# Attention rounds reordered head by head, parts stored once, expert weights loaded after the rounds

## What is computed

```python
h = _layernorm(x) * (1 + ca) + sa
qkv = h @ w_qkv + b_qkv                       # 16 heads of depth 8
q, k = _rope(q), _rope(k)
scores = einsum('bhtd,bhsd->bhts', q, k) / sqrt(8)
out = einsum('bhts,bhsd->bhtd', softmax(scores), v)
x = x + ga * (out @ w_fc + b_fc)
```

## Time and profile before

| | us |
|---|---|
| median of three runs | 1827.18 |
| the profiled execution, its own time | 1828.58 |
| its span, first to last instruction | 1826.5 |
| set-up and first rounds, to the first pass 1 | 0 to 42 |
| rounds 0 to 17 | 42 to 385 |
| experts and layer 1 | 392 to 1826.5 |

### The profile page before, as it was taken

The page is one execution under the profiler, slowest core; times in us unless marked ns, Lnnn a source line. Parts: engine busy times, 40 slices in busy tenths (PEclk is TensorE's granted clock), DMA queues, the critical chain, the costliest instruction groups (busy, mean ns, idle before and its releaser), DMA issues.

```text
span 1826.5 us, 25499 instructions
## 1 busy us (share of the span) xinstructions
PE 1659.0 (91%) x7212; PEld 1027.0 (56%) x7212; DVE 1366.2 (75%) x2636; ACT 819.6 (45%) x1533; POOL 691.8 (38%) x628
## 2 busy tenths in 40 slices
PE   3888888869989999999999999999998899899999
PEld 2455555446655656556665565655655555555555
DVE  4777777656979988979969889799698587544444
ACT  1566767657644234243352342533525543433333
POOL 2011111100002945928739469187394475000000
PEclk9989989989999999999999999999999999999999
DMA  6554445246575877677767666666671111111110
GB/s 199 152 157 129 119 111 152 89 125 215 180 207 188 222 205 204 210 209 214 215 189 203 187 188 197 189 197 204 190 194 52 41 47 52 35 57 53 52 52 23
DMA packets 172698, 269.49 MB, mean 148 GB/s; under 512 B 23748, under 2 KB 61981, under 8 KB 170053
## 3 DMA queue, kind: packets, MB, share of 16 engines
q1 hardware_dynamic: 168691, 266.33, 49.9%
q10 hardware_dynamic: 1874, 1.36, 0.2%
q0 software_dynamic: 2048, 0.79, 0.2%
HBM read 233.78 MB, written 34.62 MB: 147 GB/s over the span
## 4 chain that ended last, share of the span: by engine, by line
PE 36%; DVE 16%; issue 10%; POOL 10%; ACT 3%; DMA 3%; SPq 1%; DVEq 0%; POOLq 0%; ACTq 0%
PE psum L1528 10%; PE psum L1368 6%; POOL e_prod L1986 6%; PE psum L1370 6%; PE psum L1369 6%; PE psum L1383 5%; DVE psum L1897 4%; POOL e_phi L1986 3%; DVE e_hm L1900 2%; DVE e_vbar L1755 2%; DVE e_y L1755 1%; DVE e_state L1850 1%; DMA e_ring<-w_split 1%; PE psum L1462 1%; DMA rw<-rw_fm 1%
## 5 line engine op out<-in xcount | busy, mean ns | idle before, releaser
L1694 ACT ACTIVATE e_gu<-psum 128x512 f32<-128x512 f32 (+1 forms) x368 | 219.3, 598 | 545.5 <-PE psum L1370 284.3
L1368 PE MATMUL psum<-e_hhi,e_ring 128*128 128x512 f32 x704 | 434.0, 616 | 19.7 <-DMA e_ring<-w_split 11.5
L1383 PE MATMUL psum<-e_hm,w_d 128*128 128x512 f32 (+1 forms) x736 | 382.6, 601 | 15.0 <-DVE e_hm L1903 7.2
L1986 POOL TENSOR_TENSOR e_prod<-e_state,e_phi 128x512 f32<-128x512 f32 x256 | 353.4, 1417 | 2.4 <-POOL e_phi L1986 1.7
L1897 DVE TENSOR_TENSOR psum<-psum,rw 128x512 f32<-128x512 f32 x352 | 243.4, 692 | 90.9 <-PE psum L1370 85.1
L1935 DVE TENSOR_TENSOR e_hm<-psum,rw 128x512 f32<-128x512 f32 x256 | 174.6, 688 | 178.0 <-ACT psum L1722 176.9
L1369 PE MATMUL psum<-e_hhi,e_ring 128*128 128x512 f32 x704 | 279.0, 396 | 0.0
L1370 PE MATMUL psum<-e_hlo,e_ring 128*128 128x512 f32 x704 | 278.8, 396 | 0.0
L1900 DVE TENSOR_TENSOR e_hm<-psum,e_gu 128x512 f32<-128x512 f32 x352 | 243.5, 692 | 39.4 <-ACT e_gu L1694 15.7
L1528 PE MATMUL psum<-e_hm,w_gu 128*128 128x512 f32 x512 | 262.9, 598 | 6.6 <-DVE w_d L1916 5.5
L1722 ACT ACTIVATE psum<-psum 128x512 f32<-128x512 f32 x256 | 148.8, 582 | 254.7 <-PE psum L1370 238.8
(11 more groups left out here) (304 smaller groups left out, 2181.0 us busy)
## 6 DMA issues: line engine op xcount, KB each, us to landing
e_ring<-w_split SPq DMA_DIRECT2D x308, 256.0 KB, 4.2
rw<-rw_fm SPq DMA_DIRECT2D x192, 176.0 KB
qk_parts<-at_part SPq DMA_DIRECT2D x96, 192.0 KB, 3.1
rw<-gates_fm SPq DMA_DIRECT2D x72, 256.0 KB, 3.2
w_split<-e_ring SPq DMA_DIRECT2D x44, 256.0 KB, 2.7
rw<-rw_fm SPq DMA_DIRECT2D x64, 160.0 KB
at_qs<-qk_parts SPq DMA_DIRECT2D x16, 576.0 KB
at_ks<-qk_parts SPq DMA_DIRECT2D x16, 576.0 KB
```

Source lines behind the costliest of these rows:

```text
L1368: pe.matmul(out, w_hi, x_hi, start=first, stop=False)
L1383: mm = pe.matmul(ps[:, ACC, :], weights_at(T, WD + P * j, P)[0:rows(j), :], hm[0:rows(j), slot(j), :], start=(j == 0), stop=(j == HT - 1))
L1694: a(act_g[0:r, j % 2, :], ps[0:r, GB[j % 2], :], ACT.Silu).then_inc(silu_done, 1)
L1986: ins = tt(out[:, at], x[:, at], y[:, at], op)
```

## The change

Four things. PE's order: the scores of one head at a time, with one short piece between heads, where `pv` is cut in halves of eight matmuls and the eight output transposes in two fours. DVE and ACT follow: the normalized output is made before the maximum of head 7 and the split, the second rest after head 8, the third cut after the copy of the first maxima; ACT copies the output after exponent 2. SP's stores: each part is written once (two stores a round), and each stack is loaded by three DMAs of 24 rows; for `ks` each of them reads one part three times over, as a broadcast. The weights: no pieces in the rounds; all 16 are issued after SP's last round, once the last maxima rows are in. The cut diff:

```diff
-STACK_DMAS = 2
-OUT_DMAS = 2 * PARTS
+STACK_DMAS = 2 * PARTS
+OUT_DMAS = 2
-PIECE_ROUNDS = (0, 1, 2, 3, 13, 14, 15, 16)
...
 
-            def pv(m, j, g):
-
-                pe.wait_ge(exp_done, HEADS * m + GROUP * (g + 1))
-                if g == 0:
+            def pv(m, j, g, st):
+
+                if st == 0:
+                    pe.wait_ge(exp_done, HEADS * m + GROUP * (g + 1))
+                if g == 0 and st == 0:
                     pe.wait_ge(v_ready, m + 1)
...
                         pe.wait_ge(o_ready, m)
-                for st in range(2):
-                    for c in range(GROUP):
-                        h = GROUP * g + c
-                        mm = pe.matmul(o_ps[VW * c:VW * (c + 1), g * SEQ:(g + 1) * SEQ],
-                                       v1[:, j % BUFS, st, h, :], pt[:, h % (2 * GROUP), st, :],
-                                       start=(st == 0), stop=(st == 1), tile_position=(0, VW * c))
-                mm.then_inc(pv_done, 1)
+                for c in range(GROUP):
+                    h = GROUP * g + c
+                    mm = pe.matmul(o_ps[VW * c:VW * (c + 1), g * SEQ:(g + 1) * SEQ],
+                                   v1[:, j % BUFS, st, h, :], pt[:, h % (2 * GROUP), st, :],
+                                   start=(st == 0), stop=(st == 1), tile_position=(0, VW * c))
+                if st == 1:
+                    mm.then_inc(pv_done, 1)
 
...
                     mm.then_inc(qk_proj, 1)
-                scores(n, k, 0, 0)
-                if k == BATCH:
-                    pe.wait_ge(r0_x, 1)
-                    pe.wait_ge(max_done, HEADS * BATCH)
-                    r0_ln.pe_x(pe)
+                scores(n, k, 0)
                 if f["p1"] or f["p2"]:
...
                     mm.then_inc(vn_done, 1)
+                scores(n, k, 1)
+                if k == BATCH:
+                    pe.wait_ge(r0_x, 1)
+                    pe.wait_ge(max_done, HEADS * BATCH)
+                    r0_ln.pe_x(pe)
                 if f["tail"]:
-                    pv(n - 2, k - 2, GROUPS - 1)
-                scores(n, k, 0, 1)
+                    pv(n - 2, k - 2, GROUPS - 1, 0)
+                scores(n, k, 2)
+                if f["tail"]:
+                    pv(n - 2, k - 2, GROUPS - 1, 1)
+                scores(n, k, 3, 4)
 
...
                     for tt in range(2):
+                        if tt == 1:
+                            scores(n, k, 5)
                         for g in range(GROUPS):
...
                     mm.then_inc(ot_done, 1)
-                scores(n, k, 1)
+                    scores(n, k, 6)
+                else:
+                    scores(n, k, 5, 6)
+                if f["p2"]:
+                    pv(n - 1, k - 1, 0, 0)
+                scores(n, k, 7)
                 if k == BATCH:
...
                 if f["p2"]:
-                    pv(n - 1, k - 1, 0)
-
-                scores(n, k, 2, 0)
+                    pv(n - 1, k - 1, 0, 1)
+                scores(n, k, 8, 9)
                 if f["p1"] or f["xn"]:
...
                     mm.then_inc(xt_done, 1)
-                scores(n, k, 2, 1)
+                scores(n, k, 10)
+                if f["p2"]:
+                    pv(n - 1, k - 1, 1, 0)
+                scores(n, k, 11)
                 if k == BATCH:
...
                 if f["p2"]:
-                    pv(n - 1, k - 1, 1)
+                    pv(n - 1, k - 1, 1, 1)
+                scores(n, k, 12)
 
...
                     mm.then_inc(at_done, 1)
-                scores(n, k, 3)
+                scores(n, k, 13)
                 if f["p2"]:
-                    pv(n - 1, k - 1, 2)
+                    pv(n - 1, k - 1, 2, 0)
+                scores(n, k, 14)
+                if f["p2"]:
+                    pv(n - 1, k - 1, 2, 1)
+                scores(n, k, 15)
                 if f["tail"]:
...
 
-            def maxima(n, k, g):
+            def maxima(n, k, first, end):
                 if not live(k)["p1"]:
                     return
-                for h in range(GROUP * g, GROUP * (g + 1)):
+                for h in range(first, end):
                     dve.wait_ge(p1_done, HEADS * n + h + 1)
...
                         .then_inc(qk_ready, 1)
-                maxima(n, k, 0)
+                maxima(n, k, 0, 4)
                 if f["proj"]:
...
                     nc.vector.tensor_tensor(rest[:], qk[:], part[:, 0, :], ALU.subtract).then_inc(rest_ready, 1)
-                maxima(n, k, 1)
-                split_maxima(n, k, 0)
-                if f["proj"]:
-                    dve.wait_ge(part_ready, PARTS * (n + 2) + 2)
-                    nc.vector.tensor_tensor(rest2[:], rest[:], part[:, 1, :], ALU.subtract).then_inc(rest_ready, 1)
+                maxima(n, k, 4, 7)
                 if k == BATCH:
...
                                             ALU.mult).then_inc(a_ready, 1)
+                maxima(n, k, 7, 8)
+                split_maxima(n, k, 0)
+                maxima(n, k, 8, 9)
+                if f["proj"]:
+                    dve.wait_ge(part_ready, PARTS * (n + 2) + 2)
+                    nc.vector.tensor_tensor(rest2[:], rest[:], part[:, 1, :], ALU.subtract).then_inc(rest_ready, 1)
                 if k == BATCH:
...
                         route_stage(nc.vector, r0_steps, r0_bufs, T["gate_b"], CT, stage, r0_weighted)
-                maxima(n, k, 2)
-                maxima(n, k, 3)
+                maxima(n, k, 9, HEADS)
                 split_maxima(n, k, 1)
...
         def _(act):
-            def exps(n, k, g, part=None):
-
-                for h in heads(g, part):
+            def exps(n, k, *run_of_heads):
+
+                for h in run_of_heads:
                     act.wait_ge(p2_done, HEADS * n + h + 1)
-                    if h % GROUP == 0 and (k > 0 or g >= 2):
-
-                        act.wait_ge(pv_done, GROUPS * n + g - 1)
+                    if h % GROUP == 0 and (k > 0 or h >= 2 * GROUP):
+
+                        act.wait_ge(pv_done, GROUPS * n + h // GROUP - 1)
                     nc.scalar.activation(pt[:, h % (2 * GROUP), :, :].rearrange("p s t -> p (s t)"), ps[:, P2[h % 2], :],
...
                 if f["p2"]:
-                    exps(n - 1, k - 1, 0, 0)
+                    exps(n - 1, k - 1, 0, 1)
                 if f["p1"] or f["p2"]:
...
                     nc.scalar.activation(npart[:], ps[0:PARTS * HALF, M1, SEQ:2 * SEQ], ACT.Copy).then_inc(nrow_ready, 1)
+                if f["p2"]:
+                    exps(n - 1, k - 1, 2)
                 if f["tail"]:
...
                 if f["p2"]:
-                    exps(n - 1, k - 1, 0, 1)
+                    exps(n - 1, k - 1, 3)
                 if f["proj"]:
...
                 if f["p2"]:
-                    exps(n - 1, k - 1, 1)
+                    exps(n - 1, k - 1, 4, 5, 6, 7)
                 if k == BATCH:
                     r0_ln.act_h(act, 0, 0)
-                if f["proj"]:
-                    cut(n, k, 2)
                 if f["p2"]:
-                    exps(n - 1, k - 1, 2, 0)
+                    exps(n - 1, k - 1, 8, 9)
                 if f["p1"] or f["xn"]:
...
                         nc.scalar.activation(npart[:], ps[0:PARTS * HALF, M0, SEQ:2 * SEQ], ACT.Copy).then_inc(nrow_ready, 1)
+                if f["proj"]:
+                    cut(n, k, 2)
                 if f["p2"]:
-                    exps(n - 1, k - 1, 2, 1)
+                    exps(n - 1, k - 1, 10, 11)
                 if k == BATCH:
...
                     nc.scalar.activation(r0_e[:], ps[:, 1, 0:CT * EXPERTS], ACT.Exp, scale=-1.0).then_inc(r0_exp_done, 1)
+                if f["p2"]:
+                    exps(n - 1, k - 1, 12)
                 if f["tail"]:
...
                 if f["p2"]:
-                    exps(n - 1, k - 1, 3)
+                    exps(n - 1, k - 1, 13, 14, 15)
                 if f["tail"]:
...
 
-                sp.dma_start(stack[0:ROWS, buf, :, :], bounce[buf, q].rearrange("b a d h t -> (b a d) h t")).then_inc(stacked, 16)
+                for b in range(PARTS):
+                    if q == 0:
+                        src = bounce[buf, 0].rearrange("a d h t -> (a d) h t")
+                    else:
+                        src = bounce[buf, 1, b].unsqueeze(0).broadcast_to([PARTS, DEPTH, HEADS, SEQ])
+                    sp.dma_start(stack[b * PARTS * DEPTH:(b + 1) * PARTS * DEPTH, buf, :, :], src).then_inc(stacked, 16)
 
...
                     buf = (k + 2) % BUFS
-                    for i in range(PARTS):
-                        sp.dma_start(bounce[buf, 0, i].rearrange("a d h t -> (d h) a t"), part[:, :, 0:SEQ]).then_inc(part_out, 16)
-                    for i in range(PARTS):
-                        sp.dma_start(bounce[buf, 1, :, i].rearrange("b d h t -> (d h) b t"), part[:, :, SEQ:2 * SEQ])\
+                    for q in range(2):
+                        sp.dma_start(bounce[buf, q].rearrange("a d h t -> (d h) a t"), part[:, :, q * SEQ:(q + 1) * SEQ])\
```

(17 more changed lines are left out.)

## The result

The kernel after takes 1859.3 us (median of four runs, 1851.61 to 1876.71) beside 1826.98 for the kernel before: 1.0192 times, 95% interval 1.0135 to 1.0249. Taken again, six runs gave 1855.91 and 1.0128 (1.0099 to 1.0158). So it is slower by some 27 to 32 us, outside the forecast range.

The account below looks back on a forecast made before the run. No engine is full in rounds 0 to 17: PE and DVE idle for each other, and the clock drops. -13.9 - 2 - 4.5 + 1.5 + 1 = -17.9 from 1827.18 gives 1809.3; 2 kept back: 1811, range 1800 to 1845 (8 in 10).

Parts of the forecast that it names:

- The load of `ks`: SPq, each round: 7.3 us of data or less, hidden before the next round needs it, so nothing lost in the rounds.
- The bound on `ks`: Rival, SPq: the ks load on three engines at 16.4 GB/s becomes the limit, 21.9 us a round, 1852 us; chance 0.24.
- The ring: Chain from first cut through maxima copy, row store and load, ks load and landing back to the cut: 21.9 us a round.
- its sign: PE waiting for ks or ACT's first cut for the parts' stores, DMA share near 0.19 for many us.
- The row of rates: Measured DMA rates: 16.4 GB/s an engine for today's 72-row load, 27 each from 434 GB/s over sixteen.
- Laid out 18.2 us: One round of the new order on PE, DVE and ACT, worked out: 18.2 us for 18.82.
- the wait at L288: PE's 1.18 us wait before the output transposes, for DVE's normalized output, in each round; claimed to go.
- half of the 1.08 us as saved: Rounds: the mean's excess over round 6, 1.08 us, put down to clock drops; half taken as saved, bounds none and all.
- -13.9: Rounds 2 to 13: gain in us from order and clock, 1.16 us in each of 12 rounds, between -7.4 and -20.4.
- Out of the rounds -6.5: Rounds 1 and 15: late starts of pass 2 vanish without weight pieces in the queues, -2 and -4.5 us.
- behind them +1.5: After the last round: 16 weight pieces delay the router's weights; cost 0 to 7 us, taken as +1.5.
- The fill: First round's start, where nothing covers the ks load: between 0 and +6 us, taken as +1.

Follow-up runs that it names:

- e14_k_once: The kernel before with only k's parts stored once and loaded by three DMAs that repeat eight rows three times; 1859.8 us, ratio 1.016.
- e3_parts: The kernel before with the parts of q and k stored once and each stack loaded in three DMAs, order and weights as before; 1860.2 us, ratio 1.017.
- e2_order: The kernel after with the stores, loads and weight pieces of before, so only the new order is left; 1829.6 us, ratio 1.000.
- e13_q_once: The kernel before with only q's parts stored once and loaded by three plain DMAs; 1825.9 us, ratio 0.998.
- e1_nine: The kernel after with the ks stack loaded by nine DMAs of eight rows in place of three that repeat; 1883.4 us, ratio 1.027.
- e16_after: The kernel after, unchanged, measured again; 1855.9 us, ratio 1.013.
- e6_joined: The kernel after with both halves of each PV group and both fours of output transposes joined again; 1853.8 us, ratio 1.013.

## Why the prediction was wrong

**The load of `ks`, the step that failed.** The prediction has "all up to 8 us is covered. I take 7.3 or less, nothing in the rounds". The size was right: three engines, 81 GB/s at a share of 0.19 over sixteen, is 27 GB/s each, and the load takes 7 to 8 us. The Trainium skill, "DMA: Bandwidth & Descriptors", "Rules for kernel authors", gives at most three engines for a broadcast of three copies in the outermost dimension, and the trace agrees: share 0.19. What failed is the cover. I counted the data of `ks` against the time until head 0, and left out, in the forecast, what travels beside it: for a row store of 12 KB POOL waits 4.8 to 5.9 us in rounds 2 to 12 of e14_k_once, for 2.6 to 4.4 before, on a path with no slack (PE waited 0.79 us for these rows already), and stores of parts take up to 10.1 us to land, for 4.8. Last lines of the view of `qk_parts`, before and after (its landings are those of the stores):

```profile
DMA to landing us min/median/max: 2.1/3.1/4.8
DMA to landing us min/median/max: 2.1/2.7/10.1
```

I also counted SPq's issue at 0.32 us a load; a repeating one takes 0.69, 2.2 for the three, and so even the cover of `ks` itself fell short (issued 181.26, in use only at 191.89, 0.96 us late). The price: 30 us alone (e3_parts, e14_k_once), not 0.

**The rival that came true.** The bound on `ks` was priced at 21.9 us a round and 1852, and got 0.24. The rounds take 22.5, the time is 1856 to 1859. The ring it names is there in part (the wait of 4.33 us at the first cut is one link), and so is its sign, the share of 0.19. But the load ran at 27 GB/s an engine, not 16.4, and with that the ring's own terms give 17.2 us a round: late rows, dearer issues and the clock stand in for the slower data, so that its 1852 came out near is partly luck. The row of rates was the wrong place to decide by. (At 10 us of data its terms give 19.9 a round, not 19.4, which leaves hardly any gain in place of 1818.)

**The order.** Laid out 18.2 us; 18.5 where the clock is full (six of e2_order's rounds); the wait at L288 went, as said. The wait for the maximum at head 2 is the late one, 0.87 us where I had 0.4. But "half of the 1.08 us as saved" failed: falls went from nine to three, each dearer, and the time at the lower clock is the same (44 us for 46). In the profiled execution round 13 starts 5.6 us earlier than before (295.60 for 301.18), but the experts 0.7 us later: the last rounds, with two falls of 10 us, lose what the others gain. -13.9 came out as 0 (interval -4 to +5), and as +19 to +22 beside the late stacks, a case I had not considered.

**Weights.** Out of the rounds -6.5, behind them +1.5: -5 in all, measured -14 (-19 to -9) alone, but -6 with q once (1819.85 for 1825.91) and -7 with the order (1822.9 for 1829.6). Sign right, size right or under. The rows' waits of rounds 1 and 15, went (12.3 to 3.9 us in all). The tail was sized well: 3.02 us from the router's store to its loads for 2.34.

**Parts stored once, fewer stores.** Taken as 0; e13_q_once agrees (0.9982, 0.9964 to 1.0000).

**The fill.** Taken as +1 of 0 to 6. First pass 1 of the kernel after (timeline of PE), for 42.1 before:

```profile
44.58 0.61 PE L186 MATMUL psum<-at_ks,at_qs 72*128 72x256 bf16 x2 [8.49 <-DMA at_ks<-qk_parts]
```

+2.5 us; the wait is 6.6 longer (8.49 for 1.88), but PE reached it earlier.

## What to carry to other kernels

A transfer that is hidden by its own length can still cost its neighbours: look for small transfers on a path without slack that share its engines, and move it in time to see which of them is hit. Pay for repeated rows where they are written if the load is on the path: one plain load of 72 rows beats three that repeat eight. Test each part of a compound change alone and in pairs; here the one free edit cost some 20 us beside a bad one.

## What the runs showed of the hardware that was not expected

- A load that repeats rows takes 0.69 us to issue on SPq, a plain one 0.29 to 0.36.
- Loads of eight rows of 8 KB hold eight engines' worth of share (0.48) at 66 GB/s, 8.6 GB/s each, against 27 each for the repeating form: more engines, not more speed.
- A 12 KB store on another queue holds POOL for 4.8 to 5.9 us beside the repeating load (e14_k_once), 2.6 to 4.4 beside the plain one (before), 1.65 alone. As many of its twelve packets are late as the load keeps engines busy: three (kernel after), or eight (e1_nine).
- With PE busy for 96% of the time or more, TensorE's granted clock stayed at 1.2 GHz for up to 41 us behind a short lull in the order of short pieces (10 to 41 in the kernel after, also 3.5 and 7 in e16_after), and for 3.5 to 10 us, mostly 3.5, where the pieces were joined to runs of 16 PV matmuls and eight transposes (e6_joined).
